# A GRU chain on one core: the low-rank inputs in two 64-column places, and the set-up in the order of its loads

## The reference

```
L0: x1 = (shared_mlp(x) + sum over the top 2 of 8 experts) / 3 + x     # router with a bias from cond
L1: x2 = x1 * (2 + gate),  gate = sigmoid(silu(cond W1 + b1) W2 + b2)  # wavelets there and back cancel
L2: u = x2 a2;  mid = gelu(x2 down + u b2);  v = mid b1
    x3 = 2 x2 + mid up + v a1          # a1, b1, a2, b2: rank 8, one set per batch row, made from cond
L3: z, r = sigmoid(...);  h = tanh(x3 Wxh + (r * H) Whh);  H = (1 - z) h + z H     # 512 steps in time
    y = H Whq + bhq + x3
```

## Time and profile before

| | us |
|---|---|
| median of 3 runs (1224.37 to 1226.22) | 1224.48 |
| the profiled execution | 1227.36 |
| its span, first to last instruction | 1224.8 |

### The profile page before, as it was taken

One profiled execution on the slowest core, in us unless ns is written; L12 is line 12 of the kernel. 1 busy time (PEld: TensorE's weight loads), 2 busy tenths in 40 slices (PEclk: granted clock), 3 DMA queues, 4 the chain that ended last, 5 costly groups with the idle time before them and its releaser, 6 DMA issues.

```text
span 1224.8 us, 53989 instructions
## 1 busy us (share of the span) xinstructions
PE 1210.3 (99%) x22455; PEld 1168.0 (95%) x22455; DVE 892.0 (73%) x5771; ACT 448.8 (37%) x2253; POOL 65.6 (5%) x50
## 2 busy tenths in 40 slices
PE   7999999999999999999999999999999999999998
PEld 6799999999999999999999999999999999999975
DVE  4377777777777777777777777777777777777765
ACT  1233333333333333333333333333333333333332
POOL 2300000000000000000000000000000000000000
PEclk8999999999999999999999999999999999999999
DMA  9401100111100111110011100011111011111000
GB/s 352 179 25 29 29 14 18 29 29 29 29 24 9 28 29 29 29 29 7 25 29 29 29 29 16 16 29 29 30 29 29 4 29 29 29 29 25 3 7 10
DMA packets 42884, 43.83 MB, mean 36 GB/s; under 512 B 7416, under 2 KB 39424, under 8 KB 41360
## 3 DMA queue, kind: packets, MB, share of 16 engines
q1 hardware_dynamic: 40288, 38.91, 10.6%
q10 hardware_dynamic: 2128, 0.89, 0.3%
q0 software_dynamic: 224, 0.59, 0.2%
HBM read 35.70 MB, written 4.69 MB: 33 GB/s over the span
## 4 chain that ended last, share of the span: by engine, by line
PE 97%; DVE 1%; DMA 1%; ACT 0%; issue 0%; ACTq 0%; POOL 0%; DVEq 0%; POOLq 0%
PE bank L373 53%; PE gate_rh L373 31%; PE gate_z L373 12%; DMA xt<-in_xT 1%; ACT rg L755 0%; DVE rhp L1044 0%; DVE state L1060 0%; DVE zin L1054 0%; ACT zg L755 0%; POOL expn L344 0%; DVE zsum L1049 0%; DVE hin L1056 0%; DVE rh L1045 0%; DVE ge L945 0%; ACT pe_e L755 0%
## 5 line engine op out<-in xcount | busy, mean ns | idle before, releaser
L755 ACT ACTIVATE rg<-gate_rh 128x16 f32<-128x16 f32 x512 | 94.3, 184 | 455.6 <-PE gate_rh L373 455.6
L373 PEld LDWEIGHTS gate_rh<-state,whp 128*128 128x128 f16 x6144 | 233.2, 96 | 20.6 <-DVE state L1060 10.0
L373 PE MATMUL gate_rh<-state,whp 128*128 128x8 f16 x6144 | 248.1, 167 | 1.8 <-DVE state L1060 0.9
L373 PEld LDWEIGHTS gate_rh<-rhp,whp 128*128 128x128 f16 x6144 | 227.5, 96 | 14.0 <-DVE rhp L1044 8.0
L373 PE MATMUL gate_rh<-rhp,whp 128*128 128x8 f16 x6144 | 234.5, 167 | 0.6 <-DVE rhp L1044 0.3
L1044 DVE SCALAR_TENSOR_TENSOR rhp<-rg,hist 128x16 f16<-128x16 f32 x512 | 89.9, 176 | 157.1 <-ACT rg L755 144.2
L373 PE MATMUL gate_z<-state,whp 128*128 128x16 f16 x4096 | 179.7, 176 | 0.0
L755 ACT ACTIVATE zg<-zsum 128x16 f32<-128x16 f32 x512 | 110.6, 216 | 166.5 <-DVE zsum L1049 166.5
L373 PE MATMUL bank<-xt,rw 128*128 128x128 f32 x1024 | 165.9, 292 | 0.0
L373 PE MATMUL bank<-ge,rw 128*128 128x128 f32 x1024 | 165.2, 290 | 0.0
L1054 DVE TENSOR_SCALAR zin<-zg,nsscale 128x16 f32<-128x16 f32 x512 | 120.2, 235 | 55.4 <-ACT zg L755 37.7
(11 more groups left out here) (159 smaller groups left out, 1604.2 us busy)
## 6 DMA issues: line engine op xcount, KB each, us to landing
gates<-gates_t SPq DMA_DIRECT2D x30, 512.0 KB, 5.2
aw<-in_aw SPq DMA_DIRECT2D x4, 2048.0 KB, 23.7
out<-osb SPq DMA_DIRECT2D x32, 128.0 KB, 2.9
xt<-in_xT SPq DMA_DIRECT2D x30, 128.0 KB, 5.5
rw<-in_rw SPq DMA_DIRECT2D x2, 1024.0 KB, 11.1
sw<-in_sw SPq DMA_DIRECT2D x3, 512.0 KB, 7.8
wh<-in_wh SPq DMA_DIRECT2D x3, 256.0 KB, 13.2
wx<-in_wx SPq DMA_DIRECT2D x3, 256.0 KB, 20.2
```

The lines of the kernel that those rows point to most:

```text
L373: return pe.matmul(o, w, x, start=start, stop=stop, skip_group_check=True)
L755: return act.activation(o, i, f, **kw)
```

## The change

- `low_in_rank` takes 64 of a2b1's columns, and writes half k of the sum to partitions 64k to 64k + 63 of `low_ps`; the halves are not added there. `keep_own` masks all 128 partitions; `lows` holds b2 twice and a1 twice (second copies by two small DMAs), so the next matmul adds both halves over 128 rows.
- At s = 2 and s = 5 two passes of a chunk (`up_half`) move from `between_steps` to `between_z_h`.
- `zin` is made by a scalar_tensor_tensor with a tile `nsscale` of 16 columns, not by a tensor_scalar with a pointer.
- In the set-up: l1w1, l1w2 and aw1 go to SP's queue, up behind aw2; scores of block 1 stand behind gated_up, with fills of zeros (`WARM_*`) ahead of it; block 2's scores come from a tile of their own (`xahead`); `adapt` is cut in four parts, one for each slice of aw2; the first step is written out, with its R matmuls ahead of x3; wx is scaled by ScalarE, not by GpSimd; the last part of block 1's L0 moves into the recurrence.

```diff
--- before.py
+++ after.py
...
+WARM_CN, WARM_SHARED, WARM_GATED = 1, 4, 4
...
-        low = sb("low", [P, 2, D])
+        low = sb("low", [P, D])
+        lows = sb("lows", [P, 2, D])
...
+        xahead = sb("xahead", [P, KC, TOK])
...
-        nsscale = sb("nsscale", [P, 1])
+        nsscale = sb("nsscale", [P, KC, B])
...
             sp.dma_start(rw1[:], a["rw1"]).then_inc(l0r_in, 16)
+            sp.dma_start(l1w1[:], a["l1w1"]).then_inc(l1_in, 16)
             sp.dma_start(sw2[:], a["sw2"]).then_inc(l0o_in, 16)
+            sp.dma_start(l1w2[:], a["l1w2"]).then_inc(l1w2_in, 16)
             sp.dma_start(rw2[:], a["rw2"]).then_inc(l0o_in, 16)
+            sp.dma_start(aw1[:], a["aw1"]).then_inc(ad_in, 16)
...
             sp.dma_start(down[:], a["down"]).then_inc(l2_in, 16)
-            sp.dma_start(up[:], a["up"]).then_inc(l2_in, 16)
             load_aw2(3)
             load_aw2(0)
-            for g in range(3):
+            sp.dma_start(up[:], a["up"]).then_inc(up_in, 16)
+            for g in (R, Z, H):
                 sp.dma_start(wx[:, g], a["wx"][g]).then_inc(wx_in, 16)
...
+            sp.wait_ge(low_dve, 3)
+            sp.dma_start(lows[BR:P, 0], lows[0:BR, 0]).then_inc(lows_in, 16)
+            sp.dma_start(lows[0:BR, 1], lows[BR:P, 1]).then_inc(lows_in, 16)
...
-            pool.dma_start(l1w1[:], a["l1w1"]).then_inc(l1_in, 16)
-            pool.dma_start(l1b[:], a["l1b"]).then_inc(l1_in, 16)
-            pool.dma_start(l1w2[:], a["l1w2"]).then_inc(l1w2_in, 16)
+            pool.dma_start(l1b[:], a["l1b"]).then_inc(l1b_in, 16)
...
+            pool.wait_ge(gating, GATE_OPS + 1)
+            exp_scores((0, 2))
             pool.wait_ge(w_scaled, 6)
             pool.tensor_tensor(whp[:, 1], wrest[:], whp[:, 0], ALU.subtract).then_inc(split_w, 1)
-            pool.wait_ge(gating, GATE_OPS + 1)
-            exp_scores((0, 2))
-            pool.wait_ge(wx_in, 16 * 3)
             pool.wait_ge(scales_done, 2)
-            for g in (R, Z, H):
-                pool.tensor_scalar(wx[:, g], wx[:, g], xscale[:, g:g + 1], None, ALU.mult).then_inc(wx_scaled, 1)
...
-            def low_in_rank(x, done):
+            def low_in_rank(x, at, done):
 
                 for k in range(KC):
-                    i = mm(low_ps, a2b1[:, k], x[:, k], False, k == KC - 1)
+                    i = mm(low_ps[k * BR:(k + 1) * BR], a2b1[:, k, at * BR:(at + 1) * BR], x[:, k], False, True)
                 i.then_inc(done, 1)
 
             def mid_low(m):
                 pe.wait_ge(um_done, count(m, 1))
+                if m[1] == 1:
+                    pe.wait_ge(lows_in, 32)
                 for half in range(KC):
-                    i = mm(mid_ps[:, half], low[:, 1, half * P:(half + 1) * P], um[:], False, True)
+                    i = mm(mid_ps[:, half], lows[:, 0, half * P:(half + 1) * P], um[:], False, True)
                 i.then_inc(mid_done, 1)
 
...
-                    i = mm(mid_ps[:, half], low[:, 1, half * P:(half + 1) * P], vm[:], False, True)
+                    i = mm(mid_ps[:, half], lows[:, 1, half * P:(half + 1) * P], vm[:], False, True)
                 i.then_inc(l2_done, 1)
...
+            def first_reset_gate():
+                pr = rh_ps[0][:, 0, :, 0:B]
+                parts = state[:].rearrange("p k b a -> p k a b")
+                pe.wait_ge(st_hi, 1)
+                pe.wait_ge(st_low, 1)
+                pe.wait_ge(split_w, 1)
+                pe.wait_ge(seeded, 1)
+                recur(pr, R, 0, parts, 1)
+                recur(pr, R, 1, parts, 1)
+                recur(pr, R, 0, parts, 0)
+
+            def first_step():
+                pe.wait_ge(x3_done, 1)
+                pe.wait_ge(wx_scaled, 1)
+                project(0, R, 0)
+                project(0, R, 1).then_inc(r_done, 1)
+                pe.wait_ge(wx_scaled, 2)
+                pe.wait_ge(seeded, 2)
+                project(0, Z, 0)
+                project(0, Z, 1)
+                update_gate(0, slice(0, B)).then_inc(z_done, 1)
+                pe.wait_ge(wx_scaled, 3)
+                pe.wait_ge(rg_done, 1)
+                project(0, H, 0)
+                project(0, H, 1)
...
                 n = step_count(m, s)
+                if n == 1:
+                    first_step()
+                    return
...
-                if n == 1:
-                    for half in range(KC):
-                        project(0, Z, half)
...
-                i.then_inc(z_done, 1)
+                update_gate(par, now).then_inc(z_done, 1)
...
                         l0_out(1, "r", (6, 7))
                         pe.wait_ge(ge03_done, count(m2, 1))
+                        if m[1] < 0:
+                            set_bits(gate_rh[1])
+                            set_bits(gate_z[1]).then_inc(bits_set, 1)
...
                     if s == 2:
-                        low_in_rank(x2, u_done)
+                        low_in_rank(x2, 0, u_done)
                     if s == 3:
                         mid_low(m1)
                     if s == 5:
-                        low_in_rank(g2, v_done)
+                        low_in_rank(g2, 1, v_done)
                     if s == 6:
                         up_low(m1)
+                if has_l0:
+                    if s == 2:
+                        up_half(A1, sw1, par, 2, 0, a1_done, False)
+                    if s == 5:
+                        up_half(A3, sw3, par, 2, 0, a3_done, False)
...
-                        up_chunks(A1, sw1, par, (2, 3), a1_done, True)
+                        up_half(A1, sw1, par, 2, 1, a1_done, False)
+                        up_chunks(A1, sw1, par, (3,), a1_done, True)
                     if s == 3:
                         up_chunks(A3, sw3, par, (0, 1), a3_done, False)
                     if s == 5:
-                        up_chunks(A3, sw3, par, (2, 3), a3_done, True)
+                        up_half(A3, sw3, par, 2, 1, a3_done, False)
+                        up_chunks(A3, sw3, par, (3,), a3_done, True)
...
-            def adapt(p):
-                for slot in range(2):
-                    pe.wait_ge(ad2_in[PAIRS[p][slot]], 16)
+            def adapt(p, part):
+                slot = PAIRS[p][part]
+                pe.wait_ge(ad2_in[slot], 16)
                 for r in range(4):
                     for k in range(KC):
-                        for t in range(4):
-                            at = (PAIRS[p][t // 2] * RANK + t % 2 * 4 + r) * D
+                        for t in (2 * part, 2 * part + 1):
+                            at = (slot * RANK + t % 2 * 4 + r) * D
                             i = mm(pair_ps[p][t * SPAN:(t + 1) * SPAN], ah[:, k, SPAN - B - r * B:2 * SPAN - B - r * B],
                                    aw2[:, k, at:at + D], r == 0 and k == 0, r == 3 and k == KC - 1)
                 i.then_inc(adapt_pe, 1)
...
-            scores(m1, 1, 1)
+            warm(WARM_CN)
             pe.wait_ge(ident_in, 16)
...
             i.then_inc(setup_pe, 1)
+            warm(WARM_SHARED)
             pe.wait_ge(setup_dve, 4)
             shared_up(m0, 0)
+            warm(WARM_GATED)
             gated_up(m0, 0)
-            pe.wait_ge(l1_in, 32)
+            scores(m1, 1, 1)
+            pe.wait_ge(l1_in, 16)
...
             i.then_inc(setup_pe, 1)
+            out_shared(m0)
             pe.wait_ge(ad_in, 16)
+            pe.wait_ge(score_in, 2)
             for half in range(KC):
                 for k in range(KC):
                     i = mm(gate_z[0][:, half * B:(half + 1) * B], aw1[:, k, half * P:(half + 1) * P], cT[:, k],
                            k == 0, k == KC - 1)
             i.then_inc(setup_pe, 1)
-            out_shared(m0)
             out_47(m0)
+            pe.wait_ge(ahead_in, 16)
+            for k in range(KC):
+                i = mm(score_ps[0], xahead[:, k], rw[:, k], k == 0, k == KC - 1)
+            i.then_inc(scores_done, 1)
+            out_03(m0)
             pe.wait_ge(setup_dve, 8)
             pe.wait_ge(peaks_dve, 5)
...
-            out_03(m0)
+            shared_up(m1, 1)
             pe.wait_ge(peaks_dve, 7)
             mm(gate_rh[0][:, P:P + 4], ones4[:], peakd[:], True, True).then_inc(peaks_pe, 1)
-            shared_up(m1, 1)
-            pe.wait_ge(zeroed, 3)
+            pe.wait_ge(zeroed, 1)
             pe.wait_ge(setup_act, 3)
-            adapt(0)
+            adapt(0, 0)
             gated_up(m1, 1)
+            adapt(0, 1)
+            spread(m1)
             pe.wait_ge(low_dve, 1)
...
-            pe.wait_ge(l2_in, 32)
+            pe.wait_ge(l2_in, 16)
             mid_base(m0)
             pe.wait_ge(ready_dve, 4)
-            low_in_rank(x2, u_done)
+            for k in range(KC):
+                i = mm(low_ps[0:BR], a2b1[:, k, 0:BR], x2[:, k], False, k == KC - 1)
+            i.then_inc(u_done, 1)
+            adapt(1, 0)
...
             experts_47(m1, 1)
+            set_bits(gate_rh[0]).then_inc(bits_set, 1)
+            pe.wait_ge(low_dve, 2)
+            pe.wait_ge(um_done, 1)
```

(93 more changed lines are left out.)

69 lines of the change are left out of this document (33 added, 36 removed).

## The result

| | before | after |
|---|---|---|
| median of 12 runs on the same chips, us | 1226.61 (1224.1 to 1228.2) | 1229.14 (1226.8 to 1237.4) |
| the profiled execution, us | 1227.36 | 1227.52 |
| its span, us | 1224.8 | 1225.5 |
| VectorE busy, us | 892.0 | 865.1 |

The ratio after to before is 1.0021, 95% interval 1.0012 to 1.0031: 2.6 us slower, at the edge of what a measurement of this kernel tells from no change. The predicted difference was +2.8. Of its three terms the first fits, the second was 1.6 us too large and the set-up was put too low; that the sum fits is partly luck. The predicted time itself, 1227.3, was built on the median of three runs, 1224.48; twelve runs put the kernel before at 1226.61, and so the measured 1229.14 lies 1.8 above the prediction although the difference fits.

The account below looks back on a forecast made before the run. The tensor engine was taken to bound the kernel, holding 97% of the chain of waits. Terms +6.8 - 4.6 + 0.6 = +2.8 us, added to a 1224.5 median, gave 1227.3 us, range 1210 to 1235.

Parts of the forecast that it names:

- (a): zin in the recurrence: faster instruction lets the scan start 0.024 us earlier in 190 floor steps, -4.6 us.
- (b): Narrow low-rank inputs at filler indices 2 and 5: width changes delay H by 0.26, 60 steps x 0.114, +6.8 us.
- (c): Front of the set-up: wait for x goes, dense work starts at 7.65 at full clock; lower clock costs 1.8.
- (d): Rest of set-up: tensor engine work of 51.1 us, second reset gate near 62.5 against 62.33; +0.6 with set_bits.
- the floor: Shortest recurrence step, set by the loop through ScalarE and VectorE: 2.18 us before, 2.16 expected with the new zin.
- The point that decides: Low-rank steps: the recurrence turns slower once H's delay exceeds 0.23 us; the predicted delay was 0.26.
- Rival 2: Set-up: adapt's parts take half each, 6.9 us less, 1220.4 us; chance 0.12.
- the fours of adapt: Set-up trace: adapt's narrow passes start in fours 0.22 us apart, read as evidence against places running in series.
- places in series: Rival for low-rank inputs: two places run one after the other, H 0.37 later, 1233.9 us; 0.15 shared with other cases.

Follow-up runs that it names:

- e1: The kernel before, with only zin changed to a scalar_tensor_tensor with a whole tile of -sscale: 1219.67 us, ratio 0.9949 to the kernel before.
- e2: The changed kernel with low-rank inputs again as four full-width passes and the half chunk back between the steps: 1223.59 us, ratio 0.9979 to the kernel before.
- e5: The changed kernel with both half chunks back between the steps, only the narrow low-rank passes between Z and H: 1223.06 us in one execution.
- e3: The changed kernel with the first two of adapt's four parts joined in one run of 64 passes: 1223.94 us, ratio 0.9981 to the kernel before.
- e4: The changed kernel with full-width low-rank inputs, both adapts whole and wx scaled ahead of gelu_mid: 1216.52 us, ratio 0.9924 to the kernel before.
- e8: The changed kernel without its nine fill passes of zeros at the front of the set-up: 1227.86 us, ratio 1.0002 to the kernel before.
- e9: The changed kernel with the half chunk's two full-width passes ahead of the narrow matmuls instead of behind: 1229.75 us, ratio 1.0023 to the kernel before.
- e7: The changed kernel with probe passes of zeros of several widths added ahead of H in each block's six floor steps: 1272.19 us in one execution.
- e6: The changed kernel with both 64-column low-rank matmuls added up in one place instead of two: 1241.62 us.

## Why the prediction was right or wrong

| term | predicted | by the trace | by the runs |
|---|---|---|---|
| (a) zin | -4.6 | -5.0 | -6.3 +- 1.7 (e1 and before) |
| (b) low-rank inputs | +6.8 | +5.2 | +5.2 +- 1.7 (after and e2) |
| (c), (d) set-up | +0.6 | +1.5 | +3.7 +- 2.0 (e2 and e1) |
| sum | +2.8 | +1.7 | +2.6 |

The column of the runs is a chain, before to e1 to e2 to after, so its three steps add up to the measured sum by construction; each step's size is what it tells. The two profiled spans differ by 0.7 only (1225.5 and 1224.8), less than the traces' sum of 1.7: late steps cost 1.6 less in the execution after (last section), and some 0.6 the other way is spread over the rest.

(a) The mechanism and the size were right: ScalarE's release of 0.033 was read from another release of the same kind, and the scan now stands 0.032 behind ScalarE's `hin`. The 5.0 lies inside the runs' interval; what they may show beyond it is not explained by this step.

(b) The mechanism was right: H comes 0.247 later (predicted 0.264), and the floor at 2.157 lets 0.153 of it be taken back. The term was mis-sized by 1.6 us, through 0.017 of the sum at H and 0.010 in the step, times 60. Most of this is the prediction's own adding: its pieces as listed come to 0.80 at H, which is what was measured, and not to 0.81; and 2.18 - 0.02 + 0.26 is 2.42, not 2.427. With 0.80 and 2.157 it would have had 2.407, or +5.6. That the pieces add up so well is partly luck. One by one: entry and way out are 0.106 and 0.20, as read from the set-up; the narrow weights' own 0.05 isn't there, but the second passes of the two places start 0.15 to 0.16 after the first and not 0.11. Its sum reaches 0.48 at the end of the narrow group's way out, and it said of block 30, which has no half chunk, that the narrow passes alone take about the old 0.55 and cost nothing. Both hold: in the profile after, at index 5 of that block, H starts at 1173.64, 0.48 behind the last Z pass at 1173.155, and the step lasts 2.163, at the floor; e5 has 0.475. What it did not draw from this is that the half chunk, not the narrow form, is what costs. Those two f32 passes have one second pass at 0.21 in place of 0.11, and fill 0.32 of a stretch from which only 0.153 can be had back. The point that decides, 0.23 of delay, was passed by 0.02, and all forms tried stay above it or bring nothing.

(c) This step failed. I took the full clock beyond 8.02 because the fills were there, and gave the half clock as a bound of +1.8. It was the half clock in the profiled execution (+1.5), and in others it is worse: the half clock lasts from the start until 12.6 to 13.3 in e3, e4, e8 and e9 and until 10.2 to 10.5 in e5 to e7, with shared_up starting at 9.15 in e3. I had read one row of the kernel before as a consequence of its idle time. e1's profile, the old set-up again, has the half clock up to 19.83. So the clock at the front varies between executions, within which the new order ends its slow part earlier (10.1 to 13.3 in all its executions, with and without the fills, against 18.3 and 19.8), yet starts its dense work at it.

(d) Adapt's parts each take the whole: predicted 3.46, measured 3.58, 4 x 0.12 = 0.5 in all. e3 and e4 confirm the term by taking it away: -4.9 and -6.7 for -3.6 and -7.2. Rival 2 falls. The `set_bits` pair put 0.42 on one step, predicted 0.43. In the profiled execution the set-up is thus +1.1 at the second reset gate plus 0.4, of which 0.9 over the prediction is the clock and adapt, less waits that I had put too high.

Of the 3.7 us that the runs give the set-up, the traces show 1.5 to about 1.7 (second step's tanh at 64.6 as the mean of the six executions with the same adapt, 63.3 as that of two before, and the 0.4). The fall of the clock behind the first block adds 1.3 to 3.7 in some executions. Whether this is the rest isn't settled; the intervals would allow no rest at all.

Whether the second place waits for the first is answered by e6: taking the second place away costs two passes. With it, the first passes of both places start 0.007 apart, and then both second ones, 0.15 to 0.16 behind them. The prediction took the rule of the Trainium skill, TensorE: Matmul & The Clock Gate, Part 3, that matmuls start and end in program order, to mean that the second matmul starts only behind both passes of the first. The page doesn't say so: it draws matmuls on different tiles as overlapping, each starting about 4 ns after the one before. Taken by whole matmuls of two passes, this case's trace agrees with the order as well, as far as it can: starts and last passes both come 0.007 apart. It doesn't name the place of a pass. So the fours of adapt do not speak against the rule, and the rule did not speak for places in series.

## What to carry to other kernels

Before splitting a matmul over column places, price the change of width on both sides: here 0.2 us a round trip, whatever the size of the pass, which takes back two f32 passes. Count besides it the f32 group that the narrow one breaks in two: its second pass comes 0.1 us late once more. Ask not only what the new form costs but what it displaces onto the critical stretch, and how much of the relief elsewhere a floor lets through; the form alone was harmless, the filler moved beside it cost 5 us. When an operation runs over parallel places, cutting it into parts by place doubles its time, so cut it by passes.
